# A mixture-of-experts stage: router's products first, counts behind the first shared unit, two shared units behind the expert blocks in place of one

## The reference

```python
def _L2_ffn_ref(hidden_states, gate_w, w_gate_up, w_down, shared_gate_up, shared_down):
    E = 8; K = 2; H = 256; I = 512
    x = hidden_states.reshape(-1, orig_shape[-1])
    shared_out = _silu_and_mul(x @ shared_gate_up) @ shared_down
    router_logits = x @ gate_w
    probs = jax.nn.softmax(router_logits, axis=-1)
    topk_w, topk_i = lax.top_k(probs, K)
    topk_w = topk_w / jnp.sum(topk_w, axis=-1, keepdims=True)
    ...
    # for each expert: acc + combine[:, e] * (_silu_and_mul(x @ w_gate_up[e]) @ w_down[e])
    return (moe_out + shared_out).reshape(orig_shape)
```

## Time and profile before

| what | us |
|---|---|
| median of 3 runs | 949.21 (948.98 to 950.43) |
| span of the profiled execution, first to last instruction | 947.1 |
| median above that span | 2.1 |
| TensorE busy in the span | 819.3 (87%) |
| VectorE busy | 620.1 (65%) |
| ScalarE busy | 390.9 (41%) |
| this stage, from its first to its last instruction | 634.3 to 834.4 |
| its first block's turn of rows | 679.5 |

### The profile page before, as it was taken

How to read it: one execution, slowest core, us unless ns; L and a number is a source line. 1 busy time by engine, 2 the same in 40 slices (tenths; PEclk the granted TensorE clock), 3 DMA queues, 4 the chain that set the end, 5 groups by cost and what they waited for, 6 DMA issues and landing times. The chain is left out here.

```text
span 947.1 us, 12745 instructions
## 1 busy us (share of the span) xinstructions
PE 819.3 (87%) x4477; PEld 508.3 (54%) x4477; DVE 620.1 (65%) x1318; ACT 390.9 (41%) x665; POOL 149.4 (16%) x205
## 2 busy tenths in 40 slices
PE   5556899997899897999997997778999999779896
PEld 3253343325688563344345796445556666447675
DVE  6887888826775688788636787453167671266774
ACT  3241456682621343566775433441122222133553
POOL 1500121130020001112310000104112221100143
PEclk9866899999999987899999998999999999989998
DMA  6326300000000454200006100894201110220000
GB/s 198 105 85 194 122 8 2 2 2 1 1 1 1 148 179 157 68 2 3 1 1 128 2 1 1 287 381 150 75 23 45 51 44 30 63 93 1 1 23 24
DMA packets 49557, 64.00 MB, mean 68 GB/s; under 512 B 12534, under 2 KB 34806, under 8 KB 49494
## 3 DMA queue, kind: packets, MB, share of 16 engines
q1 hardware_dynamic: 47302, 57.52, 19.7%
q0 software_dynamic: 1872, 5.13, 1.5%
q10 hardware_dynamic: 320, 0.52, 0.2%
HBM read 50.30 MB, written 15.51 MB: 69 GB/s over the span
## 5 line engine op out<-in xcount | busy, mean ns | idle before, releaser
L855 DVE TENSOR_REDUCE at1mx<-at1ps_s 128x1 f32<-128x512 f32 (+3 forms) x152 | 90.6, 656 | 19.9 <-PE at1ps_s L757 11.1
L855 DVE TENSOR_REDUCE at0mx<-at0ps_s 128x1 f32<-128x512 f32 (+3 forms) x152 | 90.7, 656 | 19.0 <-PE at0ps_s L757 11.1
L835 ACT ACTIVATE at1probs<-at1ps_e 128x1024 f32<-128x1024 f32 (+3 forms) x96 | 73.8, 809 | 47.9 <-PE at1ps_e L778 47.6
L835 ACT ACTIVATE at0probs<-at0ps_e 128x1024 f32<-128x1024 f32 (+3 forms) x96 | 73.8, 809 | 47.0 <-PE at0ps_e L778 46.7
L1137 PE MATMUL f2ps<-gu_raw,f2xT_b 128*128 x184 | 82.9, 593 | 1.0 <-ACT f2xT_b L1224 1.0
L1242 ACT ACTIVATE f2sg<-f2ps 128x512 f32<-128x512 f32 x30 | 17.8, 597 | 130.4 <-PE f2ps L1137 100.9
L754 PE MATMUL at0ps_s<-ks,qs 96*128 96x512 bf16 (+3 forms) x192 | 58.0, 364 | 5.1 <-DMA ks<-scratch 3.6
L754 PE MATMUL at1ps_s<-ks,qs 96*128 96x512 bf16 (+3 forms) x192 | 58.0, 361 | 2.5 <-DMA ks<-scratch 1.0
L1321 DVE TENSOR_TENSOR f2h<-f2sg,f2ps 128x512 f32<-128x512 f32 x30 | 20.5, 686 | 60.5 <-ACT f2sg L1242 29.0
L1137 PEld LDWEIGHTS f2ps<-gu_raw,f2xT_b 128*128 128x128 f32 x184 | 34.8, 190 | 35.5 <-issue 34.4
L778 PE MATMUL at1ps_e<-qs,ks 99*128 99x512 bf16 (+3 forms) x192 | 46.9, 341 | 5.3 <-DMA qs<-at1rows 3.4
(11 more groups left out here) (434 smaller groups left out, 1783.5 us busy)
## 6 DMA issues: line engine op xcount, KB each, us to landing
gu_raw<-in_L_ffn_w_gate_up SPq DMA_DIRECT2D x8, 1024.0 KB, 13.2
scratch<-parts SPq DMA_DIRECT2D x8, 768.0 KB, 3.9
qs<-scratch SPq DMA_DIRECT2D x48, 128.0 KB, 2.6
ks<-scratch SPq DMA_DIRECT2D x44, 128.0 KB, 2.7
dn_raw<-in_L_ffn_w_down SPq DMA_DIRECT2D x8, 512.0 KB, 12.3
f2x_in<-slots_in SPq DMA_DIRECT2D x23, 129.0 KB, 2.0
slots_in<-in_c_empty SPq DMA_DIRECT2D x1, 2944.0 KB, 18.8
traw<-in_L_ffn_w_gate_up SPq DMA_DIRECT2D x1, 2048.0 KB, 10.0
```

The lines of the kernel that those rows point to most:

```text
L835: act.activation(probs[:, slots(v), 0:n], ps_e[:, v % SCORE_PAIRS, :, 0:n], ACT.Exp, scale=HD ** -0.5)\
L855: dve.tensor_reduce(mx[:, p % 2, lo // CH, j:j + heads, t], rows_of, AX.X, ALU.max).then_inc(s_red, 1)
```

## The change

- The router's products are issued ahead of the first unit's gate and up, and the counts behind the first unit's, in place of behind the second's.
- LATE = 2: six shared units are in front of the blocks (B0 = 6), two behind them (`BEHIND_BLOCKS`).
- The gate and up of the first late unit is split in two sides: gate ahead of the last block's down product, up behind it. The second late unit's gate and up, and both down products, follow.
- VectorE does the last block's `y_out` ahead of the late units' h. The rows read back are added first, and the four additions from PSUM come last, behind a wait on all of them.

```diff
--- before.py
+++ after.py
@@ -1038,6 +1038,7 @@
 
 BS = 128
 NB = 23
+LATE = 2
 ROW = D + 2
 DEST, WEIGHT = D, D + 1
 
@@ -1055,9 +1056,10 @@
     FT = I // P
     TC = CH // P
     SHARED = [("shared", c, f) for c in range(NC) for f in range(FT)]
-    UNITS = SHARED[:-1] + [("block", b, 0) for b in range(NB)] + SHARED[-1:]
-    B0 = NC * FT - 1
+    B0 = NC * FT - LATE
+    UNITS = SHARED[:B0] + [("block", b, 0) for b in range(NB)] + SHARED[B0:]
     LAST = B0 + NB
+    BEHIND_BLOCKS = range(LAST, LAST + LATE)
     XS, YS = 8, 4
     PAIRS = T // 2
     got = [sem(nc, own, tag + "_got%d" % i) for i in range(XS)]
@@ -1118,15 +1120,15 @@
                                     skip_group_check=True)
                 ins.then_inc(ranks, 1)
 
-            def gate_up(u):
+            def gate_up(u, sides=range(2)):
                 kind, a, f = UNITS[u]
                 if kind == "block":
                     pe.wait_ge(xe, a + 1)
                     if a == 0:
                         pe.wait_ge(*raws_ready)
-                if u >= 2:
+                if u >= 2 and 0 in sides:
                     pe.wait_ge(hs, u - 1)
-                for s in range(2):
+                for s in sides:
                     for k in range(KD):
                         o = ps[:, 2 * s + u % 2, :]
                         if kind == "shared":
@@ -1135,7 +1137,8 @@
                         else:
                             w = gu_raw[:, bass.ds(expert[a], 1), k, s * I:s * I + I].rearrange("p a n -> p (a n)")
                             ins = pe.matmul(o, xT_b[:, a % 2, k, :], w, start=(k == 0), stop=(k == KD - 1))
-                ins.then_inc(gu, 1)
+                if 1 in sides:
+                    ins.then_inc(gu, 1)
 
             def turn_x(b):
                 pe.wait_ge(got[b % XS], 16 * (b // XS + 1))
@@ -1176,13 +1179,15 @@
                                     skip_group_check=True)
                 ins.then_inc(used, 1)
 
-            def late_down():
-
-                pe.wait_ge(hs, LAST + 1)
-                pe.wait_ge(he, NB)
+            def late_down(u):
+
+                pe.wait_ge(hs, u + 1)
+                if u == LAST:
+                    pe.wait_ge(he, NB)
+                f = UNITS[u][2]
                 for t in range(TC):
-                    ins = pe.matmul(ps_o[:, t, :], h[:, LAST % 2, t * P:t * P + P], sh[1][:, FT - 1, :],
-                                    start=(t % 2 == 0), stop=(t % 2 == 1), skip_group_check=True)
+                    ins = pe.matmul(ps_o[:, t, :], h[:, u % 2, t * P:t * P + P], sh[1][:, f, :],
+                                    start=(u == LAST and t % 2 == 0), stop=(f == FT - 1 and t % 2 == 1), skip_group_check=True)
                 ins.then_inc(used, 1)
 
             def find_expert(b):
@@ -1195,10 +1200,10 @@
             for u, (kind, a, f) in enumerate(UNITS[:LAST]):
                 if u == B0:
                     turn_x(0)
+                if u == 0:
+                    router_products()
                 gate_up(u)
                 if u == 0:
-                    router_products()
-                if u == 1:
                     count()
                 if B0 - 2 <= u < LAST - 2:
                     find_expert(u + 2 - B0)
@@ -1213,9 +1218,14 @@
                     down(u - 2 - B0)
             turn_h(LAST - 1)
             down(NB - 2)
-            gate_up(LAST)
+            gate_up(LAST, (0,))
             down(NB - 1)
-            late_down()
+            gate_up(LAST, (1,))
+            for u in BEHIND_BLOCKS:
+                if u > LAST:
+                    gate_up(u)
+                    late_down(u - 1)
+            late_down(BEHIND_BLOCKS[-1])
 
         @block.scalar
         def _(act):
@@ -1245,9 +1255,10 @@
                 if u > B0:
                     h_part(a - 1)
             h_part(NB - 1)
-            act.wait_ge(gu, LAST + 1)
-            act.wait_ge(hs, LAST - 1)
-            act.activation(sg[:, LAST % 2, :], ps[:, LAST % 2, :], ACT.Silu).then_inc(sgs, 1)
+            for u in BEHIND_BLOCKS:
+                act.wait_ge(gu, u + 1)
+                act.wait_ge(hs, u - 1)
+                act.activation(sg[:, u % 2, :], ps[:, u % 2, :], ACT.Silu).then_inc(sgs, 1)
 
         @block.vector
         def _(dve):
@@ -1328,25 +1339,23 @@
                         tern.step(dve, steps // TERN_STEPS, steps % TERN_STEPS)
                         steps += 1
             y_out(NB - 2)
-            dve.wait_ge(sgs, LAST + 1)
-            dve.wait_ge(used, LAST - 1)
-            dve.tensor_tensor(h[:, LAST % 2, :], sg[:, LAST % 2, :], ps[:, 2 + LAST % 2, :], ALU.mult).then_inc(hs, 1)
             y_out(NB - 1)
+            for u in BEHIND_BLOCKS:
+                dve.wait_ge(sgs, u + 1)
+                dve.wait_ge(used, u - 1)
+                dve.tensor_tensor(h[:, u % 2, :], sg[:, u % 2, :], ps[:, 2 + u % 2, :], ALU.mult).then_inc(hs, 1)
             dve.wait_ge(added, NC)
-            dve.wait_ge(used, LAST + 1)
-            for t in range(TC):
-                ins = dve.tensor_tensor(m.x[:, TC + t, :], ps_o[:, t, :], m.x[:, TC + t, :], ALU.add)
-            ins.then_inc(added, 1)
-            dve.wait_ge(added, NC + 1)
             for q in range(PAIRS):
                 dve.wait_ge(back[q], 32)
                 for i in range(2):
                     if i == 1:
-                        dve.wait_ge(sums, q + 1)
+                        dve.wait_ge(sums, 2 * q + 1)
                     tiles = slice(2 * q, 2 * q + 2)
-                    ins = dve.tensor_tensor(m.x[:, tiles, :], y_back[:, i, tiles, :], m.x[:, tiles, :], ALU.add)
-                    if i == 0:
-                        ins.then_inc(sums, 1)
+                    dve.tensor_tensor(m.x[:, tiles, :], y_back[:, i, tiles, :], m.x[:, tiles, :], ALU.add).then_inc(sums, 1)
+            dve.wait_ge(used, LAST + LATE)
+            dve.wait_ge(sums, 2 * PAIRS)
+            for t in range(TC):
+                dve.tensor_tensor(m.x[:, TC + t, :], ps_o[:, t, :], m.x[:, TC + t, :], ALU.add)
 
         @block.sync
         def _(sp):
```

## The result

The changed kernel took 944.88 us (median of 9 runs, 940.13 to 949.33) against 950.43 us for the kernel before, timed beside it (9 runs, 948.37 to 956.07): ratio 0.9941 with a 95% interval of 0.9916 to 0.9965, 3.3 to 8.0 us. Faster, as forecast, but by 5.6 us where the sum said 10.8, and the median lies 3.7 us above the range's upper end. A second set of 12 runs of the same kernel gave 944.76 against 950.77 (0.9933, 0.9910 to 0.9956).

What follows compares the result with a forecast made beforehand. Matmul work bounds the middle; the front and tail hold idle and slow-clock time. 10.6 us at block 0 plus 0.25 in the tail made 10.8; 947.1 - 10.8 + 2.1 gave 938.4 us, range 936.7 to 941.2.

Steps and rivals of the forecast that it cites:

- (a): Front, router's products first: VectorE's start moves 3.51 us earlier, from 641.54 to 638.0.
- (b): Front, counts behind the first unit: TensorE waits for nothing; the idle 3.53 us and the slow stretch's 1.80 us go.
- (c): Front with six units: TensorE asks for block 0's rows at 667.8 against 679.51, 11.7 us earlier.
- the rule weighed: TensorE's clock in the front: throttled is the default, so it could fall once more; sum 9.0 in place of 10.8.
- (d): Block 0's rows: their load moves by 3.5 us only, block 0 starts 10.6 us earlier, TensorE waits some 1 us.
- The late Silu: Front, ScalarE's Silu of unit 4, 3.3 us late: if it comes again, the fifth down starts 0.9 us late, covered.
- (e): Tail: the moved unit's 5.16 us go where TensorE idled for 12.28 us; 0.25 us gained.
- 1: Rival: the clock falls once in the front, behind the products or at the wait for rows; 1.80 us, 940.2; chance 0.10.
- 2: Rival: the tail gives back, PSUM additions last but the read-back starts no earlier; 940.1; chance 0.06.
- 3: Rival: block 0's rows are not late, TensorE alone sets the start; 937.4; chance 0.08.
- 5: Rival: POOL's front scatters slow by 0.80 us each beside other traffic, making it slower than before; 951.3; chance 0.03.
- 4: Rival: VectorE's routing chain stays where it was, held by something else; block 0 starts 7.2 us earlier; 941.8; chance 0.04.

Runs made afterwards that it cites:

- e1: The kernel before with only the router's products moved ahead of the first unit and the counts behind it, seven units in front, old tail; 948.45 us, ratio 0.9977.
- e9: The changed kernel with about 1.0 us of unused VectorE work added at the end of the stage; 943.61 us, ratio 0.9919.
- e10: The changed kernel with seven wide bf16 products, results unused, added among the router's products; 942.08 us, ratio 0.9912.
- e8: The changed kernel with the four PSUM additions put ahead of the eight of the rows read back, as before; 945.52 us, ratio 0.9951.
- e11: The changed kernel with about 1.7 us of unused VectorE work added at the end of the stage; 944.87 us, ratio 0.9941.
- e6: The changed kernel with the router's products spread between unit 0's wide products and the counts between unit 1's sides; 943.94 us, ratio 0.9933.
- e2: The changed kernel with the router's products and counts back in their old places, keeping two late units and the new tail; 946.04 us, ratio 0.9945.
- profiles 2 and 3: Second and third profiled executions of the kernel before, nothing changed; single runs, 948.03 and 947.71 us.

## Why the prediction was right or wrong

**(a) Router first: order right, size wrong.** VectorE's start came 5.18 us behind the stage's start, not 3.7, since the clock fell while the products ran. In e1 and e9, where the fall came later, it was 3.95 and 3.97, and even these are 0.3 us behind the forecast.

**(b) Counts without a wait: wrong.** They waited for a first gate and up of 5.63 us in place of 3.51. From (a) and (b) together the chain to the rows is 3.5 us later than forecast, first scatter 14.12 in place of 10.6: to 0.05 us where it was in the kernel before. Where the fall came at 2.4 us, the router's move gained the rows nothing. In e10, where no fall came, the first scatter was at 11.71 with the filling.

**(c) and the rule weighed: this is the step that failed.** The sum took the clock at its upper level in the whole new front, with one fall as a rival at 0.10. All five profiles of the changed front (the changed kernel twice, e8, e9, e11) have a fall in it, and so has every kernel in which the products stood together in the first 7 us, but for the kernel before. So the term that the sum put at nothing measured 3.3 us at the turn, and e10 shows that it is the clock: with wide products among the thin ones, the edges lying as before, there was no fall and the turn came at 35.47 in place of 37.91. The price was under-sized as well, 3.3 us at the turn against 1.80, because the slowed products head the longest chain (products, choice, counts, places, scatters, load), whereas the price came from a pair that only TensorE waited for. The Trainium skill's statement (TensorE: Matmul & The Clock Gate, Part 1: The HAM clock gate), that the lower clock is the default and activity lifts it, agrees with e6 and e10, where wide products among the thin ones kept 1.00. The evidence that I took against it, a clock of 1.00 in the earlier trace rows, was one order of work with wide products on both sides of the thin ones, and e2, with the same order there, did fall.

**(d) Rows late next: right.** TensorE waited for the load in all five profiles of the changed front, and 35.74 + 2.17 gives the turn. The late Silu was covered by nothing and cost nothing: it did not recur.

**The baseline.** The 1.16 us of the late addition were in one profile of three. It didn't enter the forecast time of the new front, but it made the old one 1.2 us too long. Against profiles 2 and 3, block 0 came earlier by 43.97 - 37.94 = 6.0 us, not by 45.2 - 34.6 = 10.6; 3.3 of the difference is the clock and 1.2 this.

**(e) Tail: right in its mechanism, 0.1 us or nothing in place of 0.25.** The moved unit cost nothing there: TensorE still has 7.00 us without work at the end, 12.28 before. The first read-back addition came 146.8 us behind the turn, 148.3 before: 1.5 us nearer, not 1.7, and the PSUM additions took 1.4 of that back.

**Later stages: not in the sum.** They took 115.7 in both profiles of the changed kernel, 112.4 to 114.0 in the kernel before: 1.7 us given back against profiles 2 and 3, one more low stretch. With nothing gained in the tail against those two, 6.0 - 1.7 = 4.3 us, inside the 3.3 to 8.0 of the runs. The profiles don't stand for all runs (e9 shows the same front at 36.38), so the split of the 5.6 us stays this rough. That the low stretches cost this time is read from where the profiles part; what decides how many of them come, and how often each number does in the runs, stays open.

**Rivals.** 1 came true, at nearly twice its price; its chance of 0.10 was too low. 2, 3 and 5 did not: the read-back came earlier, the rows were late, and the scatters kept their 0.96 us. The sharing of ports that 5 cites is not tested by that, since VectorE's h products beside the scatters have one input in PSUM. 4 named the right outcome, a chain to the rows that stays where it was, for a wrong reason: VectorE did start 2.1 us earlier, and the slow gate and up ahead of the counts took the same 2.1 back. That its 7.2 us at block 0 are close to the measured 45.21 - 37.91 = 7.3 is luck. The range left out what it should have held, the first rival at its true price; the kernel's runs alone spread over 9 us.

## What to carry to other kernels

Thin products (8 columns here) put together, even with TensorE busy nearly throughout, at the head of a chain can bring TensorE's clock down just where everything waits for them; put wide work among them, useful or not, and look at the granted clock of that stretch in more than one execution. When a move spends the slack of one chain, price the slow clock along the whole chain that hangs on it, not by the pair of products that showed it. And take a baseline from two or three executions: one odd wait of 1.2 us in a single profile went straight into a forecast.

## What the hardware showed that I had not expected

The later stages, with the same instructions, took between 112.4 and 115.7 us over the fourteen profiles, in values that repeat (112.4 to 112.5 four times, 114.0 to 114.5 six times, 115.6 to 115.7 four times), and the values go with none, one or two low stretches of 3.4 us inside them. A microsecond gained or lost ahead of a stage can so change what the stages behind it take, as e11 shows. Idle of 3.5 us on TensorE had a slow pair behind it in all three profiles of the kernel before (6.96 us in each in place of 5.16) and none in e2 (5.26 us), although the order of work there was the same.
